# Packing the part numbers of a count build two by two, and moving one table's bias from TensorE to VectorE

## The chip, the cores and the metric

The kernel runs on one core of a Trainium2 chip. Its time is the device time of one execution in microseconds (us). A core has five engines that matter here: TensorE (PE; its weight loads are PEld), VectorE (DVE), ScalarE (ACT), GpSimd (POOL) and SyncE (SP, which only issues transfers). Each engine has a sequencer that reads its instructions, does the register arithmetic itself and passes the rest on to the engine's queue; records of the sequencers carry a q (PEldq, SPq). The engines meet through semaphores.

## The reference

Four graph networks run one after the other on the same graph of 6250 nodes with 256 values each and 100000 edges. The edges are sorted by target. The first network is the one whose first table the change touches:

```python
h = jnp.maximum(_layernorm(x, axis=-1), 0.0)
h = h @ W_in + b_in
for l in range(n_layers):
    agg = jax.ops.segment_sum(h[src], dst, num_segments=n) / deg
    h = jax.nn.relu(agg @ W_agg[l] + h @ W_self[l] + b_hid[l])
return h @ W_out + b_out
```

The kernel folds `W_in` into `W_agg[0]` and `W_self[0]`, so the first table is relu(layernorm(x)) @ (W_in W_agg) + b_in W_agg. The second term is `b_agg`, one row of 256 values that stands in all 128 partitions.

## The kernel before

**The count build.** The sums over edges of five layers are computed as dense products with a matrix of edge counts, `adj`, which is the same in all of them and is built once, in device memory. Rows and columns of the matrix are cut into 784 blocks of 8 target nodes (16 x 392 columns wide when folded onto 128 partitions), and 24 extra parts for blocks with very many edges: 808 parts. The edges come in 782 chunks of 128. Each pair of a chunk and a block that meet is one step, 1592 in all. For a step VectorE makes two one-hot operands, `hot_key` (128 edges x 128 row keys, made for eight steps at a time, L2304) and `hot_j` (128 edges x 392 columns, L2309), and TensorE multiplies them into one of four PSUM banks (L1498). The bank is that of the step's part: part z goes to bank z mod 4. Behind each such matmul TensorE waits until ScalarE has evicted enough parts, and then makes the next bank ready with a small matmul of two columns (L1487). When the last step of a part is done, ScalarE copies its bank into one of eight slots of `staged` (L1723) and SyncE stores the slot into `adj` (L732).

**Registers.** Which part a step belongs to depends on the edges, so it is known only at run time. The numbers lie as one row of 32-bit words, one word a step, in `step_part`, which is a piece of the buffer `g_x` (the profile shows it under that name). TensorE's sequencer loads 16 of them into 16 registers, once at step 0 and once at step 16 of a turn (L1493), and computes from them the bank and the wait (L1494, L1498, L1487). ScalarE and SyncE load eight words each for every eight parts (L1718, L728).

**Turns.** All engines walk the steps in turns of 32 (`build`, through `by_meets`): 50 turns, of which the first, the last two and some of GpSimd's are written out and the others are a loop. Beside the steps each turn does one of the 49 tiles (128 nodes) of the first table, at fixed steps. On TensorE: the transposes `in_T` at step 12, `in_P2` (s_hT times the folded W_agg, into PSUM bank 5) in two halves at steps 29 and 30, the bias as a matmul of a row of ones with `b_agg` behind the second half (L1214), and `in_P3` at steps 1 and 2 of the next turn (L1221). On VectorE: `in_h` at step 4, `in_hT` at step 28, and at steps 18, 20 and 22 of the next turn `in_hi` (L2086: the rounded part of the result), `in_low` (L2065: the rest) and `in_own` (L2070). GpSimd stores the tile at step 28. VectorE may be at most 16 steps ahead of TensorE, since `hot_j` has 16 buffers.

After the build come the dense products (L1352), which TensorE starts when all parts are evicted and the last tile is done.

## Time and profile before

| | |
|---|---|
| median of 3 runs | 7671.14 us (7663.33 to 7676.74) |
| the profiled execution | 7667.53 us |
| its span | 7665.8 us, 108469 instructions |
| TensorE busy | 6321.0 us, 82% of the span |
| VectorE busy | 3412.8 us, 45% |
| ScalarE busy | 1651.3 us, 22% |
| GpSimd busy | 2239.8 us, 29% |
| share of the chain that ended last | TensorE 59%, VectorE 11%, issue 8% |

The span is the profiled execution from its first instruction to its last. Busy times are of the engines, not of their sequencers: an engine whose sequencer is loading a register counts as idle. The build takes about the first 1004 us of the span.

### The profile page before, as it was taken

The numbers are of one execution on the slowest core, as the hardware profiler recorded it, in microseconds if no ns is written. First come the engines' busy times: TensorE is split into PE (matmuls) and PEld (weight loads), VectorE is DVE, ScalarE is ACT, GpSimd is POOL, SyncE is SP. The second block draws the span as 40 slices with busy tenths as digits, with TensorE's granted clock in tenths as the row PEclk, the third lists the DMA queues.
The fourth block names the chain that finished last, engine by engine and source line by source line (L and its number), as shares of the span: only waits on it lengthen the run. The fifth ranks groups of instructions, "written<-read, shape, count | busy, mean of one in ns | idle before, by whom it ended". The sixth has DMA issues, their size and how long they took to land.

```text
span 7665.8 us, 108469 instructions
## 1 busy us (share of the span) xinstructions
PE 6321.0 (82%) x29032; PEld 4993.3 (65%) x29033; DVE 3412.8 (45%) x9453; ACT 1651.3 (22%) x4349; POOL 2239.8 (29%) x2541
## 2 busy tenths in 40 slices
PE   5877799999999999766676765999999966777677
PEld 3555477778887777655555554777787755555555
DVE  7766666661111222355555566122233324444443
ACT  1344410000000111111111113132233332222222
POOL 1000010001001111366666652000111116666664
PEclk8887799999999999878877887999999988878887
DMA  4566777788779777533333336988977753333332
GB/s 138 181 228 242 256 284 261 256 299 312 273 277 343 262 257 256 184 83 83 85 82 84 83 90 200 333 291 294 354 249 244 243 181 97 102 100 99 100 100 75
DMA packets 606869, 1525.79 MB, mean 199 GB/s; under 512 B 72808, under 2 KB 248915, under 8 KB 606612
## 3 DMA queue, kind: packets, MB, share of 16 engines
q1 hardware_dynamic: 472803, 1129.19, 41.8%
q0 software_dynamic: 133824, 393.46, 17.0%
q8 instruction: 143, 2.34, 0.1%
q14 instruction: 99, 0.80, 0.0%
HBM read 1206.47 MB, written 316.80 MB: 199 GB/s over the span
## 4 chain that ended last, share of the span: by engine, by line
PE 59%; DVE 11%; another core or an unknown queue 11%; issue 8%; DMA 6%; DVEq 2%; ACT 2%; SPq 1%; POOL 0%; ACTq 0%; POOLq 0%
PE psum L1352 33%; PE psum L1498 4%; PE psum L1198 4%; PE psum L1646 3%; PE psum L1618 2%; PE psum L1549 2%; DMA slab<-adj 2%; DVE hot_j L2309 2%; DVE acc L2547 2%; DMA g_own<-own_dram 2%; PE psum L1630 1%; PE psum L1537 1%; PE psum L1193 1%; PE psum L1286 1%
## 5 line engine op out<-in xcount | busy, mean ns | idle before, releaser
L1352 PE MATMUL psum<-X,slab 128*128 128x512 f32 x12495 | 3111.2, 402 | 74.9 <-DMA slab<-adj 41.3
L1352 PEld LDWEIGHTS psum<-X,slab 128*128 128x128 f32 x12495 | 2347.7, 191 | 608.5 <-DVE g_x L2374 89.7
L2547 DVE TENSOR_TENSOR acc<-acc,psum 128x264 f32 (+1 forms) x1660 | 702.8, 423 | 1068.8 <-PE psum L1646 353.0
L1498 PE MATMUL psum<-hot_j,hot_key 128*128 128x392 bf16 x1592 | 570.9, 431 | 164.2 <-DVE hot_j L2309 109.4
L1012 POOL DMA_DIRECT2D table<-s_tab x147 | 80.4, 547 | 1910.8 <-DVE s_tab L2065 1910.8
L1537 PE MATMUL psum<-node_tabs,onehot_t 128*128 x1660 | 274.7, 305 | 378.3 <-ACT onehot_t L1822 348.2
L1537 PEld LDWEIGHTS psum<-node_tabs,onehot_t 128*128 128x128 f32 x1660 | 274.0, 248 | 420.6 <-issue 414.3
L1102 POOL DMA_INDIRECT ring<-gat_table,idx_slot x420 | 415.7, 990 | 261.2 <-ACT idx_slot L1817 138.1
L1102 POOL DMA_INDIRECT ring<-rel_table,idx_slot x420 | 412.6, 982 | 250.2 <-ACT idx_slot L1817 137.7
L1723 ACT CAST staged<-psum 128x392 fp32r<-128x392 f32 x808 | 373.0, 489 | 522.3 <-PE psum L1498 497.0
L1498 PEld LDWEIGHTS psum<-hot_j,hot_key 128*128 128x128 bf16 x1592 | 235.7, 148 | 321.7 <-issue 236.2
L2309 DVE TENSOR_SCALAR hot_j<-iota_j,node_tabs 128x392 bf16<-128x392 bf16 x1592 | 411.2, 318 | 73.7 <-PE psum L1498 73.6
L2353 DVE TENSOR_TENSOR node_tabs<-node_tabs,slab 128x896 f32<-128x896 f32 x343 | 374.5, 1092 | 139.2 <-DMA slab<-adj 129.1
L1618 PEld LDWEIGHTS psum<-hT,wbuf 128*128 128x128 f32 x2064 | 383.5, 234 | 48.4 <-ACT hT L1974 2.6
L2065 DVE TENSOR_TENSOR s_tab<-psum,s_tab 128x256 fp32r<-128x256 f32 x196 | 83.1, 424 | 724.3 <-ACT s_tab L1690 724.3
L1618 PE MATMUL psum<-hT,wbuf 128*128 128x128 f32 x2064 | 375.0, 315 | 1.4 <-ACT hT L1974 1.4
L1685 ACT COPY s_hT<-psum 128x256 f32<-128x256 f32 x273 | 101.7, 373 | 1189.5 <-PE psum L1193 1189.5
L1198 PE MATMUL psum<-wbuf,s_hT 128*128 128x256 f32 (+1 forms) x1484 | 336.9, 363 | 0.0
L1487 PE MATMUL psum<-node_tabs 128*128 128x2 bf16 x1593 | 292.7, 184 | 14.2 <-ACT staged L1723 14.0
L1198 PEld LDWEIGHTS psum<-wbuf,s_hT 128*128 128x128 f32 x1484 | 274.9, 190 | 44.4
L1549 PE MATMUL psum<-ring,onehot 128*128 128x264 f32 x840 | 288.9, 481 | 16.7 <-DVE ring L2567 16.7
L1646 PE MATMUL psum<-ring,onehot 128*128 128x256 f32 x840 | 274.0, 420 | 20.6 <-DMA ring<-rel_table,idx_slot 20.3
(426 smaller groups left out, 8124.2 us busy)
## 6 DMA issues: line engine op xcount, KB each, us to landing
slab<-adj SPq DMA_DIRECT2D x383, 1344.0 KB, 6.7
slab<-adj SPq DMA_DIRECT2D x313, 896.0 KB, 6.2
adj<-staged SPq DMA_DIRECT2D x808, 196.0 KB, 1.9
X<-table SPq DMA_DIRECT2D x32, 1792.0 KB, 13.4
table<-s_tab POOLq DMA_DIRECT2D x196, 256.0 KB, 3.5
g_own<-own_dram POOLq DMA_DIRECT2D x35, 896.0 KB, 8.1
own_dram<-s_out POOLq DMA_DIRECT2D x196, 128.0 KB, 5.1
acc<-zero_rows SPq DMA_DIRECT2D x2, 6600.0 KB, 27.4
```

What stands on the lines that cost most here:

```text
L1102: nc.gpsimd.indirect_dma_start(out=to, out_offset=None, in_=tab, in_offset=bass.IndirectOffsetOnAxis(ap=idx_slot[:, r * HALF + u:r * HALF ...
L1198: last = nc.tensor.matmul(ps[:, 0:n], s_hT[:, q, :], w(q), start=(q == 0), stop=(q == Q - 1))
L1352: last = nc.tensor.matmul(sums_of(j), slab[:, slab_at(c), u, j * P:(j + 1) * P], X[:, x_at(p, d), :], start=(d == 0), stop=(d == KT - 1))
L1498: nc.tensor.matmul(psum[:, bass.ds(own, 1), 0:J].rearrange("p o j -> p (o j)"), hot_key[:, s % KEYS // AT_ONCE, :, s % AT_ONCE], hot_j[:, ...
L1537: last = nc.tensor.matmul(ps_log[:, v, :], onehot_t[:, v, :], dst_tab[:, bass.ds(tiles[v], 1), :].rearrange("p t h -> p (t h)"), start=Tru ...
L1549: nc.tensor.matmul(psum[:, v, 0:GW], onehot[:, r * HALF + v, :], homes[r][:, v, :], start=True, stop=True).then_inc(sem("mm"), 1)
L1618: last = nc.tensor.matmul(psum[:, bank, b * P:(b + 1) * P], wbuf[:, q, at:at + P], hT[:, q, :], start=(q == 0), stop=(q == Q - 1))
L1646: nc.tensor.matmul(psum[:, u % GB, 0:D], onehot[:, u, :], homes[r][:, v, 0:D], start=True, stop=True).then_inc(sem("mm"), 1)
L1723: nc.scalar.copy(staged[:, r, :], psum[:, (r + 1) % RING, 0:J]).then_inc(sem("evicted"), 1)
L2309: V.tensor_scalar(hot_j[:, s % HOT, :], iota_j[:], edge_now[:, s:s + 1], None, op0=ALU.is_equal).then_inc(sem("hot"), 1)
L2353: V.tensor_tensor(slab_sum, slab_sum, of[u], ALU.add).then_inc(sem("slab_summed" if u == SIZES[c] - 1 else "slab_partly"), 1)
L2547: V.tensor_tensor(a, a, psum[:, bank, 0:w], ALU.add).then_inc(sem("summed"), 1)
```

## The change

The row of part numbers is packed: the numbers of two steps, which are equal or differ by one, are added into one 16-bit word of a new row `pair_part` (one VectorE operation on one partition, ahead of the build). From a sum s the two numbers come back as s // 2 and (s + 1) // 2. TensorE loads 16 such words once a turn, at step 0, and takes each step's number from them with one more operation on the register.

The bias matmul of the first table goes. In its place VectorE adds `b_agg` to the product as it reads it out of PSUM, into the buffer `s_xn` (new stage `in_sum`, at step 17 of the next turn, ahead of `in_hi`); `in_hi` and `in_low` read `s_xn` then. TensorE's next `in_P2` waits for `in_sum` where it waited for `in_low`.

```diff
+                pair_part = sb("pair_part", [1, PAIRS], I16, scope=late)
...
                     if q == 0:
                         pe.wait_ge(*ev("in_hT", t + 2))
-                        pe.wait_ge(*ev("in_lo", t + 1))
-                    nc.tensor.matmul(PS1_IN, s_hT[:, q, :], cols(W["in", "agg"], D)(q), start=(q == 0), stop=False)
+                        pe.wait_ge(*ev("in_sum", t + 1))
+                    last = nc.tensor.matmul(PS1_IN, s_hT[:, q, :], cols(W["in", "agg"], D)(q), start=(q == 0), stop=(q == Q - 1))
                     if q == Q - 1:
-                        nc.tensor.matmul(PS1_IN, ones[0:1, :], b_agg[0:1, :], start=False, stop=True).then_inc(sem("in_P2"), 1)
+                        last.then_inc(sem("in_P2"), 1)
...
-                    if s % NOW == 0:
-                        pe.load(zs, step_part[0:1, bass.ds(t * BUILD + s, NOW)])
-                    z = pe.snap(zs[s % NOW], min_val=1, max_val=LEAD + ENDED)
+                    if s == 0:
+                        pe.load(zs, pair_part[0:1, bass.ds(t * NOW, NOW)])
+                    if s % 2 == 0:
+                        both = pe.snap(zs[s // 2])
+                    z = pe.snap((both + s % 2) // 2, min_val=1, max_val=LEAD + ENDED)
...
-            pe.wait_ge(*ev("step_part", 16))
+            pe.wait_ge(*ev("pair_part", 1))
...
-                low("in", PS1_IN, 0, t)
+                low("in", s_xn[:], 0, t)
+
+            def in_sum(t):
+                dve.wait_ge(*ev("in_P2", t + 2))
+                dve.wait_ge(*ev("in_lo", t + 1))
+                V.tensor_tensor(s_xn[:], PS1_IN, b_agg, ALU.add).then_inc(sem("in_sum"), 1)
...
-                dve.wait_ge(*ev("in_P2", t + 2))
+                dve.wait_ge(*ev("in_sum", t + 2))
                 dve.wait_ge(*ev("in_tab0", t * 16 + 16))
-                V.tensor_copy(s_tab[:, 0, 0:D], PS1_IN).then_inc(sem("in_hi"), 1)
-
-            in_stages = [(4, in_h), (28, in_hT), (BUILD + 18, in_hi), (BUILD + 20, in_low), (BUILD + 22, in_own)]
+                V.tensor_copy(s_tab[:, 0, 0:D], s_xn[:]).then_inc(sem("in_hi"), 1)
+
+            in_stages = [(4, in_h), (28, in_hT), (BUILD + 17, in_sum), (BUILD + 18, in_hi), (BUILD + 20, in_low), (BUILD + 22, in_own)]
...
+            of_pair = step_part.rearrange("p (n two) -> p n two", two=2)
+            V.tensor_tensor(pair_part, of_pair[:, :, 0], of_pair[:, :, 1], ALU.add).then_inc(sem("pair_part"), 1)
```

Three places in the order of the instructions. The line numbers of the changed kernel are three to ten higher. An ISA row is a register instruction of the sequencer. First TensorE in the body of the loop, from the end of step 15 to the start of step 16, before:

```order
L1498 MATMUL psum<-hot_j,hot_key 128x392
L1487 ISA [waits evicted]
L1487 MATMUL psum<-node_tabs 128x2
L1493 ISA
L1493 TENSOR_LOAD g_x
L1494 ISA
L1498 ISA [waits hot]
```

and the same place after:

```order
L1503 MATMUL psum<-hot_j,hot_key 128x392
L1490 ISA [waits evicted]
L1490 MATMUL psum<-node_tabs 128x2
L1498 ISA
L1503 ISA [waits hot]
```

The load and its set-up are gone; the number of register instructions of a step is the same. Then TensorE at steps 29 and 30 of the loop, before:

```order
L1212 MATMUL psum<-wbuf,s_hT 128x256 [waits tile_lo,tile_hT]
L1494 ISA
L1498 MATMUL psum<-hot_j,hot_key 128x392
L1487 ISA [waits evicted]
L1487 MATMUL psum<-node_tabs 128x2
L1212 MATMUL psum<-wbuf,s_hT 128x256
L1214 MATMUL psum<-pbuf,ones 128x256
L1494 ISA
```

and after:

```order
L1215 MATMUL psum<-wbuf,s_hT 128x256 [waits tile_sum,tile_hT]
L1503 ISA
L1503 MATMUL psum<-hot_j,hot_key 128x392
L1490 ISA [waits evicted]
L1490 MATMUL psum<-node_tabs 128x2
L1215 MATMUL psum<-wbuf,s_hT 128x256
L1498 ISA
```

The bias matmul is gone (each of these rows runs as two matmuls on the array), and the first half waits for `tile_sum`. Last VectorE at steps 16 to 22 of the loop, before:

```order
L2309 TENSOR_SCALAR hot_j<-iota_j,node_tabs 128x392 x2
L2085 ISA [waits tile_P2]
L2086 CAST s_tab<-psum 128x256 [waits tile_tab0]
L2309 TENSOR_SCALAR hot_j<-iota_j,node_tabs 128x392 x2
L2065 TENSOR_TENSOR s_tab<-psum,s_tab 128x256 [waits tile_hi]
```

and after:

```order
L2319 TENSOR_SCALAR hot_j<-iota_j,node_tabs 128x392
L2086 TENSOR_TENSOR s_xn<-psum,pbuf 128x256 [waits tile_lo,tile_P2]
L2319 TENSOR_SCALAR hot_j<-iota_j,node_tabs 128x392
L2095 ISA [waits tile_sum]
L2096 CAST s_tab<-s_xn 128x256 [waits tile_tab0]
L2319 TENSOR_SCALAR hot_j<-iota_j,node_tabs 128x392 x2
L2070 TENSOR_TENSOR s_tab<-s_xn,s_tab 128x256 [waits tile_hi]
```

One operation more, and a wait of VectorE's sequencer on its own engine's result, one `hot_j` behind it.

## Rows read from the trace of the kernel before

**Rows 1.** Timeline of TensorE at the build's two ends: start us, us taken, instruction.

```profile
99.41 1.22 PE L1214 MATMUL psum<-pbuf,ones 1*128 1x256 f32 x2
...
1004.13 0.77 PE L1352 MATMUL psum<-X,slab 128*128 128x512 f32 x1
```

**Rows 2.** Windows: length, busy PE, PEld, DVE, ACT, POOL, PEclk, DMA share, GB/s.

```profile
115.60:599.10 483.50, 395.24 (x2128) 260.91 (x2129) 336.09 (x1207) 187.57 (x397) 31.52 (x57) 0.85 0.53 191
599.10:993.60 394.50, 306.31 (x1512) 191.96 (x1513) 239.94 (x857) 184.97 (x410) 29.58 (x49) 0.76 0.71 251
181.70:190.30 8.60, 6.41 (x40) 4.41 (x38) 7.33 (x27) 1.95 (x4) 1.08 (x2) 0.97 0.42 157
190.30:198.40 8.10, 8.04 (x37) 5.13 (x38) 4.66 (x17) 1.98 (x5) 0.00 (x0) 0.61 0.27 99
```

**Rows 3.** Timeline around the mid load of turn 5: start us, us taken, instruction.

```profile
187.44 0.39 PE L1498 MATMUL psum<-hot_j,hot_key 128*128 128x392 bf16 x1
...
187.79 0.39 PE L1498 MATMUL psum<-hot_j,hot_key 128*128 128x392 bf16 x1
...
188.12 1.01 DVE L2309 TENSOR_SCALAR hot_j<-iota_j,node_tabs 128x392 bf16<-128x392 bf16 x4
...
189.37 1.01 DVE L2309 TENSOR_SCALAR hot_j<-iota_j,node_tabs 128x392 bf16<-128x392 bf16 x4
...
190.36 0.55 PE L1498 MATMUL psum<-hot_j,hot_key 128*128 128x392 bf16 x1 [2.17 <-DVE hot_j L2309]
```

**Rows 4.** Register instructions by source line: duration ns min/median/max, first and last start.

```profile
L1494 PEldq FUSED_REGOPS  x1570: 47/94/108, 100.2 to 1003.6; - x197
...
L1487 PEldq FUSED_REGOPS  x1592: 98/100/124, 100.0 to 1003.7; - x199
```

**Rows 5.** TensorE's register loads, L1493: all of them, then single ones.

```profile
L1493 PEldq TENSOR_LOAD <-g_x x100: 1102/1840/3278, 98.4 to 999.5; - x100
L1493 PEldq FUSED_REGOPS  x47: 47/47/47, 121.9 to 964.0; - x47
...
L1493 PEldq TENSOR_LOAD <-g_x x1: 1912/1912/1912, 188.1 to 188.1; - x1
...
L1493 PEldq TENSOR_LOAD <-g_x x1: 1615/1615/1615, 122.0 to 122.0; - x1
...
L1493 PEldq TENSOR_LOAD <-g_x x1: 1913/1913/1913, 587.2 to 587.2; - x1
...
L1493 PEldq TENSOR_LOAD <-g_x x1: 3278/3278/3278, 607.2 to 607.2; - x1
...
L1493 PEldq TENSOR_LOAD <-g_x x1: 2975/2975/2975, 964.1 to 964.1; - x1
...
L1493 PEldq TENSOR_LOAD <-g_x x1: 1385/1385/1385, 113.9 to 113.9; - x1
...
L1493 PEldq TENSOR_LOAD <-g_x x1: 1752/1752/1752, 617.3 to 617.3; - x1
```

**Rows 6.** Timeline, the bias pair near the head of turn 6.

```profile
197.33 0.69 PE L1214 MATMUL psum<-pbuf,ones 1*128 1x256 f32 x2
```

**Rows 7.** Other register loads by source line: one 16-bit word, six 32-bit words.

```profile
L898 SPq TENSOR_LOAD <-rows_row x83: 3/15/711, 6297.0 to 7621.5; - x83
...
L2823 DVEq TENSOR_LOAD <-turn_row x42: 762/1405/1425, 6298.4 to 7593.6; - x42
```

**Rows 8.** Evictions from 599 to 994 (groups), SyncE's loads, two of SyncE's stores.

```profile
L1723 ACT CAST staged<-psum 128x392 fp32r<-128x392 f32 x410 | 185.0, 490 | 207.8 <-PE psum L1498 185.4 <-DMA adj<-staged 17.2 <-issue 3.1
...
L728 SPq TENSOR_LOAD <-part_to x101: 724/761/1632, 84.8 to 987.2; - x101
...
637.50 0.92 SPq L732 DMA_DIRECT2D adj<-staged  x2
```

**Rows 9.** VectorE operations by source line: duration ns min/median/max, start, form.

```profile
L2086 DVE CAST s_tab<-psum x49: 416/419/422, 105.5 to 978.6; 128x256 fp32r<-128x256 f32 x49
...
L2353 DVE TENSOR_TENSOR node_tabs<-node_tabs,slab x343: 1081/1092/1140, 1005.4 to 1707.7; 128x896 f32<-128x896 f32 x172
```

More of the change, by code:

```diff
@@ L87, in build @@
     assert BTURNS == T + 1 and SB2 * P - MEETS + ENDED + MORE < ELSEWHERE
+    PAIRS = SB2 * P // 2
+    assert MEETS % 2 == 0 and BTURNS * NOW <= PAIRS
     KT = PARTS * DG // P
@@ L505, in build @@
                              ("cuts", 1), ("bound_read", 1), ("cuts_read", 1), ("z_rows", 1), ("parts_out", 1), ("marks", 1), ("x_ve", 1), ("more_rows", 1),
-                             ("b_self", 1), ("rows2_f", 2), ("x_rstd", 1), ("chunk_i", 1), ("edge_f", 2), ("turn_row", 1), ("w_att", 2 * Q),
+                             ("b_self", 1), ("rows2_f", 2), ("x_rstd", 1), ("chunk_i", 1), ("pair_part", 1), ("edge_f", 2), ("turn_row", 1), ("w_att", 2 * Q),
                              ("amax", 1), ("gdiag", 1), ("dst_tab", 1), ("zs_clamped", 1), ("bn_ve", 1), ("bn_shift", 1),
```

2 rows, old and new, of the table TILE_EVENTS are left out of this document.

## The prediction

> **What bounds the kernel now.** I read the page's busy shares first: TensorE 82% of the span, VectorE 45%. So TensorE is the engine to look at, but the share is a mean over stages. The change touches only the count build, the first stage of steps, from 98.3 to 1004.1 us; its last matmuls run straight into the first dense one at 1004.13, with no idle time noted before it [rows 1], so what the build gives up the whole kernel gives up. I then cut the build into its turns of 32 steps. 28 turns fill 115.6 to 599.1 (17.27 us each), the next 20 fill 599.1 to 993.6 (19.73 us each) [rows 2].
>
> What ends last in a turn is not the array but TensorE's sequencer. In a plain stretch one step follows another every 0.35 us (187.44, 187.79) [rows 3]; the sequencer spends 0.094 us and 0.100 us of it on two register instructions [rows 4], and the rest in the spacings around them. It never rests in the first 28 turns. Into this row of small pieces two register loads per turn are set, each of 16 words: one at the turn's head, one at its step 16. While one runs the sequencer passes on nothing. The mid load shows as a hole: the matmul of 187.79 is followed by the next at 190.36, 2.57 us where 0.35 is normal; the load in it took 1.912 us [rows 3, 5]. The row names VectorE's hot_j as what ended the wait, but the four that end at 190.4 are those of steps 28 to 31 (in_hT, which stands ahead of step 28, runs just before them), needed twelve steps later: the load is the cause. The head load is hidden in part: the array still has in_P2's matmuls and the bias pair queued, which runs at 197.33 [rows 6] while the head load of 196.9 is under way.
>
> **Part 1, the mid load goes.** Sixteen packed words now serve 32 steps, so of two loads and two small set-ups per turn one of each goes; the regops per step stay at two (the order shows the same count, one more operand computation inside an existing one). A removed load is worth itself plus 0.16: its set-up of 0.047 [rows 5] and the two spacings around it. Read one by one, the 28 mid loads of the first stretch have a mean of 2.23 us (first 1.615, last 1.913), the 20 of the second 2.55 us (first 3.278, last 2.975); the heads have 1.39 and 1.64 (first of each: 1.385, 1.752) [rows 5]. Sum: 28 x (2.23 + 0.16) = 66.9, 20 x (2.55 + 0.16) = 54.2, and for the first and last turn, 2 x (1.11 + 0.16) = 2.5. Together 123.6 us if nothing takes any of it back.
>
> **Part 2, what takes it back.**
> *Head loads get longer.* The same 16 registers take 1.1 us at best and up to 3.28 [rows 5]. The long ones lie where VectorE runs all through them (from 188.12 to 190.4 it makes eight hot_j with in_hT between [rows 3]); during head loads it mostly waits. VectorE has 12.0 us of work per turn (336.09 / 28) [rows 2]; in a turn of 15 us it is busy 80% of it instead of 70%, and what it used to catch up during the mid load it will catch up during the head load. I take half of the way from head to mid: 0.45 us x 48 = 21.6 us. Bounds: 0, and the whole way, 0.88 x 48 = 42.
> *16-bit words.* Before never loads sixteen of them. Nearest rows: one 16-bit word into SyncE's sequencer, 0.015 us typical; six 32-bit words into VectorE's, 1.405 us, 0.23 a word [rows 7]; sixteen 32-bit words into TensorE's, 1.10 at best. If the bytes count, half of 1.1 is saved, 50 x 0.55 = 27 us; if the registers count, nothing changes. The ends are 27 us gained and, by VectorE's word (sixteen in 3.75 us), 48 x (3.75 - 1.5) = 108 us lost. I take 0, by the row of the same engine.
> *The late turns.* From 599 on, 410 evictions in 394.5 us go through ScalarE (0.49 us each) and SyncE, which issues a store for each, 0.59 us apart at the closest (two of 0.33 in 0.92), and loads its own registers every eight, 0.76 to 1.63 us [rows 8]. 51 octets x (8 x 0.59 + 0.76 to 1.63 + some 0.35 for its loop) = 297 to 342 us. That leaves 53 to 97 us of slack, and the saving would eat 54 of it. The stores have then less room to catch up. Late turns are already 2.5 us longer than early ones though their mid loads are only 0.3 longer: TensorE waits there for other things too. I take 12 us off, bounds 0 and 36.
> *Bias pair.* It goes: two matmuls, 0.69 us together and 0.6 in the array's pace [rows 6], in which the array, not the sequencer, worked; the sequencer passes matmuls on in no time that shows. In the head the array is idle or about to be while the load runs, so taking 0.6 us of array work out of the head makes the hole behind it longer, not the turn shorter. Value 0; bounds 0 and, if the array were the limit in the 20 late turns, 20 x 0.6 = 12 us gained.
> *VectorE's new in_sum.* One more 128x256 operation of 0.42 us per turn [rows 9], some 0.335 of it in the engine's pace, plus some 0.1 for a wait of its sequencer on its own result (hot_j operations are queued behind it and TensorE waits for them four steps later at the soonest, with 8 to 16 steps of lead). 12.0 + 0.43 = 12.5 us in turns of about 15: hidden. If that cover were gone it would cost 0.43 x 49 = 21. in_hi and in_lo now read SBUF; I leave them at their 0.42 [rows 9] (bounds 0 and half of it, hidden either way), so 0.
> *Start.* The packing, 1 partition x 832, is bounded by the 256-element cast, 0.42, and the 896-element addition, 1.09 [rows 9]; I take 0.95, near the addition. It stands ahead of the first hot_j on VectorE, but there the array was busy with in_P2 and the bias (99.41 for 1.22 us) until the first step [rows 1], of which the bias is gone. 0.5 us lost.
> Sum: 123.6 - 21.6 - 12 - 0.5 = 89.5 us. The profiled execution took 7667.5 (span 7665.8 and 1.7 around it), which is 3.6 below the median of 7671.1. 7667.5 - 89.5 = **7578 us**, 1.2% less than before.
>
> **Two rules against the rows.** The Trainium skill, "Runtime: NRT & Kernel Launch", section "Instruction fetch mechanics", puts a register load at some 200 ns for each register even in bulk; by it the shortest load here would be 3.2 us, and the trace has 1.1 us [rows 5], so it is not this price, but its form (registers, not bytes) would make the 16-bit words worth nothing, which is my value.
> In the trace the granted clock was 0.97 in the half turn before the mid load of 188.1 and 0.61 in the one behind it [rows 2], and the matmul went from 0.39 to 0.55 us [rows 3]: the array idled 2.17 us and fell to 1.2 GHz. The Trainium skill, "TensorE: Matmul & The Clock Gate", section "Part 1: The HAM clock gate", says that idling throttles the array and work releases it; the trace agrees, and by it a head hole made longer could lower the clock for the in_P3 matmuls that follow; that is the slow side of the second rival.
>
> **Rivals.**
> R1, nothing is taken back: head loads keep 1.4 to 1.6 and the late turns follow. 123.6 - 0.5 = 123 us less, 7544; with the higher clock after step 16 or shorter 16-bit loads down to 7520. For it: the shortest loads, 1.10, are heads. Against: VectorE's share rises.
> R2, the late turns hardly gain, because eviction and store pace them (or the clock falls at the head and the array lags, which delays evictions): 66.9 + 2.5 - 21.6 - 0.5 and a third of 54 left, 65 us, 7602; with heads as long as mid loads 7622. For it: the 2.5 us by which late turns are longer, and ring buffers of four banks that let TensorE run no more than three parts ahead of ScalarE. Against: at least 53 us of slack.
> R3, VectorE becomes the bound: with the mid load gone its lead is not refilled, and TensorE waits for hot. Price: turns of 15.5 to 16 instead of 14.9, some 40 us of the gain, 7618. For it: 12.5 of 15 us. Against: it idles over 2 us a turn.
> R4, slower: the 16-bit load. Place: the head of each of 50 turns, where the sequencer stands still. If a word costs what VectorE's row says, with 0.3 us to start, a load takes 4.05 us: 2.55 more in 48 turns is 122 against 111 gained (123.6 - 12 - 0.5), so about 7679. It decides from a head load of 3.8 us. Against: SyncE's 16-bit words in 0.015 us [rows 7].
> R5, the change doesn't do what it says: the order shows one load per turn, so only its size is open.
>
> **How the numbers follow.** Forecast (7560 to 7600) 0.48; R1 0.22; R2 0.16; R3 0.07; R4 0.04; the rest, mixtures near no change, 0.03. The range, to leave out at most 2 in 10: from 7530, which keeps most of R1, to 7622, the end of R2. 0.2% is 15 us, about what a measurement of this kernel tells from no change. Faster by more: 0.93; within: 0.03; slower: 0.04.
>
> **What would show it.** Right: one load per turn, starts about 15 us apart in the first 28 turns; no hole at step 16, hot_j matmuls there at 0.39 and a granted clock over 0.9 in the second half turn; head loads of 1.8 to 2.1; 28 turns in about 430 us and 20 in 360 to 370; the dense stage beginning near 915; the rest of the kernel unchanged in length. Wrong: head loads over 3 us (R4); turns of 15.5 and more with TensorE waiting for hot_j (R3); late turns over 19 us with waits for ScalarE (R2); or the dense stage waiting for slabs once the build ends sooner.

## The result, and the profile after

The changed kernel is slower: 7828.94 us (median of 4 runs, 7809.72 to 7832.88) against 7667.24 (4 runs, 7658.87 to 7676.74), a ratio of 1.0206, 95% interval 1.0184 to 1.0227. Forecast were 7578 us, a range of 7530 to 7622, and 0.04 for slower. The profiled execution took 7809.72 us, 142.2 more than that of before. Of these the build itself, from the first step's matmul to the last's, makes 134.7 (903.2 to 1037.9); it begins 2.4 us later (100.6, now 103.0), and what follows the last step is 5 us longer (6662 to 6667).

First the row that answers to [rows 5], then those of [rows 4]. The changed kernel's trace by source line; columns: ns min/median/max, first and last start.

```profile
L1496 PEldq TENSOR_LOAD <-pair_part x50: 3789/4595/6402, 98.7 to 1125.8; - x50
...
L1498 PEldq FUSED_REGOPS  x774: 41/146/165, 103.6 to 1140.2; - x194
...
L1503 PEldq FUSED_REGOPS  x1194: 132/141/162, 102.8 to 1140.8; - x199
its engine sat idle before it (us, times) until:
  issue: 575.4, 619
  DVE hot_j L2319: 3.2, 1
...
L1490 PEldq FUSED_REGOPS  x1592: 98/100/118, 103.0 to 1141.0; - x199
```

There are half as many loads, but the shortest takes 3.79 us and the median 4.6, where the shortest was 1.10 and the median 1.84. The number of these register instructions is the same (3582 in the build, before and after), but one of a step's went from a median of 94 ns to 141 or 146. Under L1503 stands what ended the idle time ahead of the steps' matmuls (us, times): "issue", TensorE's own sequencer, 575.4 us, and `hot_j` 3.2. The same two lines of the kernel before read:

```profile
  issue: 285.8, 414
  DVE hot_j L2309: 109.4, 65
```

The array waits twice as long for its sequencer, and for VectorE no more.

The same windows as [rows 2], turns 1 to 28 and 29 to 48, of the changed kernel: length, busy times of PE, PEld, DVE, ACT, POOL, then PEclk, DMA share, GB/s.

```profile
121.40:677.90 556.50, 407.04 (x2073) 255.75 (x2073) 336.50 (x1232) 187.10 (x397) 31.28 (x57) 0.84 0.46 166
677.90:1131.00 453.10, 327.23 (x1475) 194.68 (x1475) 243.70 (x877) 186.29 (x410) 29.54 (x49) 0.73 0.62 219
```

A turn takes 19.88 us instead of 17.27 in the first 28, and 22.66 instead of 19.73 in the next 20. VectorE and ScalarE are busy for as long as before. How the hole looks, in TensorE's timeline at the head of a turn (start us, us taken, instruction, idle time before it and what ended it):

```profile
190.87 0.68 PE L1215 MATMUL psum<-wbuf,s_hT 128*128 128x256 f32 x2
...
191.58 0.36 PE L1503 MATMUL psum<-hot_j,hot_key 128*128 128x392 bf16 x1
191.78 0.17 PE L1490 MATMUL psum<-node_tabs 128*128 128x2 bf16 x1
196.33 0.54 PE L1503 MATMUL psum<-hot_j,hot_key 128*128 128x392 bf16 x1 [4.38 <-issue]
196.67 0.21 PE L1490 MATMUL psum<-node_tabs 128*128 128x2 bf16 x1
196.74 1.20 PE L1224 MATMUL psum<-wbuf,s_hT 128*128 128x256 f32 x2
```

And windows of the same place: the stretch ahead of the hole, the hole, the two `in_P3` steps behind it, and what follows; under them, in a fence of its own, the `in_P3` steps of the kernel before.

```profile
187.00:191.20 4.20, 3.91 (x22) 2.64 (x22) 4.20 (x17) 1.13 (x3) 0.00 (x0) 1.00 0.52 191
191.20:196.20 5.00, 0.75 (x6) 0.37 (x4) 1.55 (x7) 0.33 (x1) 0.00 (x0) 0.93 0.11 40
196.20:199.20 3.00, 2.87 (x9) 1.90 (x10) 0.00 (x0) 0.49 (x1) 0.00 (x0) 0.50 0.00 0
199.20:203.50 4.30, 4.30 (x28) 2.49 (x27) 3.33 (x12) 1.00 (x3) 0.19 (x1) 0.63 0.25 93
```

```profile
196.80:200.00 3.20, 3.20 (x19) 2.09 (x18) 1.07 (x5) 0.88 (x2) 0.00 (x0) 1.00 0.15 56
```

Two things are to be seen. In the five microseconds of the hole VectorE is busy for 1.55, and 40 GB/s are moved: the load is long with little else going on (VectorE is busy for a mean of 24% of each of the 50 loads). And behind the hole the granted clock is 0.50 (the lower level, 1.2 GHz) where it was 1.00 at the same place before, so that `in_P3`'s pair takes 1.20 us. In steps 0 and 1 of all turns the clock had a mean of 1.00 in the first 28 turns and 0.81 in the next 20; after the change it is 0.52 and 0.50 (means over the turns). In steps 16 to 27 of the early turns it went the other way, from 0.57 to 0.98, and yet these steps take 5.13 us instead of 4.61: the array is faster there and waits for its sequencer.

Measured at the steps' matmuls, a turn splits as follows (mean us from one step's matmul to the next; step 15 carries the old mid load, step 31 the head load):

| steps | before, turns 1-27 | after | before, turns 29-47 | after |
|---|---|---|---|---|
| 28-31, head with load | 3.67 | 6.91 | 4.65 | 8.39 |
| 0-1, `in_P3` | 1.56 | 2.73 | 2.06 | 2.80 |
| 15, mid load | 2.87 | 0.45 | 3.17 | 0.50 |
| 2-14, 16-27 | 9.13 | 9.74 | 9.92 | 10.93 |
| turn | 17.23 | 19.82 | 19.80 | 22.62 |

Times 28 and 20 turns: head +166 us, `in_P3` at the lower clock +48, mid load -121, plain steps +37; together +130 of the build's 134.7.

### The profile page after: what moved, and what is told of

It is laid out like the page before. It is cut to its first block, busy times and chain, and to the rows that moved or that the text cites. A ratio compares the mean times of both kernels' runs of the same rounds, so it can differ in the third digit from the quotient of the medians.

```text
span 7808.0 us, 108317 instructions
## 1 busy us (share of the span) xinstructions
PE 6355.8 (81%) x28934; PEld 4991.3 (64%) x28935; DVE 3417.2 (44%) x9503; ACT 1651.7 (21%) x4349; POOL 2236.9 (29%) x2541
## 3 DMA queue, kind: packets, MB, share of 16 engines
q8 instruction: 145, 2.38, 0.1%
## 4 chain that ended last, share of the span: by engine, by line
PE 58%; DVE 12%; another core or an unknown queue 11%; issue 9%; DMA 5%; DVEq 2%; ACT 2%; SPq 1%; POOL 0%; ACTq 0%; POOLq 0%
PE psum L1355 33%; PE psum L1201 4%; PE psum L1651 3%; PE psum L1503 3%; PE psum L1554 3%; DVE hot_j L2319 2%; PE psum L1623 2%; DMA slab<-adj 2%; DVE acc L2559 2%; PE psum L1635 2%; PE psum L1542 2%; PE psum L1224 1%; PE psum L1196 1%; PE psum L1289 1%
## 5 line engine op out<-in xcount | busy, mean ns | idle before, releaser
L1503 PE MATMUL psum<-hot_j,hot_key 128*128 128x392 bf16 x1592 | 603.5, 425 | 263.1 <-issue 230.7
L1503 PEld LDWEIGHTS psum<-hot_j,hot_key 128*128 128x128 bf16 x1592 | 236.7, 149 | 451.8 <-issue 344.7
L2070 DVE TENSOR_TENSOR s_tab<-psum,s_tab 128x256 fp32r<-128x256 f32 x147 | 62.5, 425 | 725.7 <-ACT s_tab L1695 725.7
L2314 DVE TENSOR_TENSOR hot_key<-iota_keys,key_at 128x1024 bf16<-128x1024 bf16 x199 | 136.6, 686 | 390.4 <-PE psum L1503 389.9
```

The source lines that it names most:

```text
L1503: nc.tensor.matmul(psum[:, bass.ds(own, 1), 0:J].rearrange("p o j -> p (o j)"), hot_key[:, s % KEYS // AT_ONCE, :, s % AT_ONCE], hot_j[:, ...
```

## The experiments

**How they are compared.** The groups of runs (e1 to e4, e5 to e8, e9 to e12, e13 to e15, e16 to e18) ran on different occasions, on three chips, each beside the kernel before: its median was 7610, 7658, 7670, 7616 and, for the last group, 7181 us. The occasion counts and not only the chip, since one chip gave both 7670 and 7181. The difference lies behind the build: from the last step to the end e11 takes 6670 us and e17 6191. Its cause isn't known. So times are compared by their ratios; the build's length and the steps are from one profiled execution each. Where the sequencer sets the pace the steps agree from chip to chip: steps 16 to 27 of the early turns take 5.45 us in e1, in e5 and in e9, which ran on three chips. Lengths where the array works at either clock need not. All variants but e2 and e10 hold TensorE's part number at zero or more with a register operation, `max(number, 0)`; e1 is the control that shows what this costs, and all have such an operation on ScalarE.

| run | what it is | ratio, 95% | build us | load ns min/median/max |
|---|---|---|---|---|
| before | | 1 | 903.2 | 1102/1840/3278 x100 |
| after | | 1.0206 [1.0184, 1.0227] | 1037.9 | 3789/4595/6402 x50 |
| e1 | before + max per step | 1.0140 [1.0119, 1.0160] | 1006.3 | 1102/1631/3297 x100 |
| e2 | after, unsigned words | 1.0205 [1.0183, 1.0226] | 1037.2 | 3789/4604/5986 x50 |
| e3 | after, 32-bit pair words | 1.0035 [1.0022, 1.0048] | 917.5 | 1102/1360/1949 x50 |
| e4 | e1, 16-bit numbers | 1.0546 [1.0523, 1.0569] | 1307.3 | 3793/4822/7001 x100 |
| e5 | e1, one word further on | 1.0539 [1.0522, 1.0557] | 1312.4 | 3799/4852/7207 x100 |
| e9 | e1, two words further on | 1.0536 [1.0519, 1.0554] | 1308.5 | 3798/4746/7580 x100 |
| e6 | e1, one load of 32 words | 1.0091 [1.0071, 1.0110] | 961.7 | 2130/2642/4255 x50 |
| e7 | e1, halves of 32-bit words | 1.0168 [1.0151, 1.0185] | 1017.8 | 1102/1116/1932 x50 |
| e8 | e1, bias on VectorE | 1.0121 [1.0104, 1.0138] | 970.1 | 1102/1634/3115 x100 |
| e10 | e2, bias on TensorE | 1.0201 [1.0184, 1.0218] | 1036.5 | 3790/4590/6311 x50 |
| e11 | e1, both loads moved | 1.0074 [1.0057, 1.0091] | 949.2 | |
| e12 | e11, bias on VectorE | 1.0078 [1.0062, 1.0095] | 946.0 | |
| e13 | e3, shifts for divisions | 1.0155 [1.0134, 1.0175] | 1016.7 | 1102/1140/1855 x50 |
| e14 | e11, max and wait per pair | 1.0088 [1.0063, 1.0112] | 960.3 | |
| e15 | e14, one operation fewer | 1.0087 [1.0070, 1.0105] | 950.2 | |
| e16 | e3, max in a block | 0.9987 [0.9975, 0.9998] | 886.0 | 1102/1381/2197 x50 |
| e17 | e11, max in blocks | 0.9999 [0.9990, 1.0009] | 903.8 | |
| e18 | e17, bias on VectorE | 1.0013 [1.0002, 1.0025] | 903.3 | |

### What makes the load long

**e1_held**, the control.

```diff
+pe.reg_alu(z_held, zs[s % NOW], 0, op=ALU.max)
-z = pe.snap(zs[s % NOW], min_val=1, max_val=LEAD + ENDED)
+z = pe.snap(z_held, min_val=0, max_val=LEAD + ENDED)
```

> The kernel before, with one more register operation on TensorE in each of the 1600 steps of the build (the part number is first held at zero or more: max(number, 0)), and one on ScalarE ahead of its wait, which has slack. It is the control for all kernels derived from the one before, and prices a register operation. Theory A (TensorE's own instruction stream sets the pace of a step, so each register operation counts): 1600 x 0.048 us = +77 us, 7744 us. Rival (a step has slack between its matmuls, an operation more is hidden): 7667 us, no change.

1.0140, some 107 us, more than expected: on TensorE one operation per step, nothing else, and the build is 103 us longer. A plain step has no slack for its sequencer; it goes from 0.35 to 0.43 us. That is some 60 of the 103 us. About 50 more lie in steps 28 to 31, 0 and 1, where the fp32 matmuls run at the lower clock more often (the mid hole gives 10 back): the clock in turns 1 to 28 falls from 0.85 [rows 2] to 0.70:

```profile
116.50:669.00 552.50, 473.92 (x2128) 275.59 (x2129) 335.16 (x1202) 188.22 (x396) 31.40 (x57) 0.70 0.46 167
```

**e2_after_u16**: `pair_part` of type uint16 instead of int16.

> The changed kernel with its 16-bit words unsigned instead of signed (and one register operation more on ScalarE). It is the control for the kernels derived from the changed one. Both theories (16-bit words are read one by one; or the unpacking and the place of the load are the cause): 7829 us within 15, 16-word loads of 4.6 us. Only if the sign extension of a 16-bit word is what costs would it fall, towards 7680 us.

1.0205, as the changed kernel. The sign costs nothing.

**e3_pair32**: the changed kernel with 32-bit pair words.

```diff
-pair_part = sb("pair_part", [1, PAIRS], I16, scope=late)
+pair16 = sb("pair16", [1, PAIRS], I16, scope=late)
+pair_part = step_part[:, 0:PAIRS]              # 32-bit, copied from pair16
...
-both = pe.snap(zs[s // 2])
+pe.reg_alu(z_held, zs[s // 2], 0, op=ALU.max)
+both = pe.snap(z_held)
```

> The changed kernel with its pair words held as 32-bit numbers: the same one load of 16 registers at a turn's head, the same unpacking, and max(word, 0) on each even step (800 register operations more, +40 us by 0.05 each). Theory A (a load costs by how it reads memory, and 16-bit words are read one by one): the load falls from 4.6 us to the 1.4 to 1.6 us of a head load before, 50 x 3.1 = -155, and +40: about 7715 us (7690 to 7740). Rival B (the load is long because of its place at the head, or because of what VectorE and the DMAs do there, and the rest is the unpacking): the load stays at 4 us or more, 7829 + 40 = 7869 us.

The load is back at 1.36 us, the ratio at 1.0035, below e2 by 1.7% although it has 796 register operations more. The place at the head, the packing and VectorE's work in the build are the same in both (one copy of the row ahead of the build is added): rival B falls.

**e4_two_u16**: the control with the numbers as 16-bit words, two loads per turn as before.

```diff
-pe.load(zs, step_part[0:1, bass.ds(t * BUILD + s, NOW)])
+pe.load(zs, step16[0:1, bass.ds(t * BUILD + s, NOW)])      # uint16
```

> The first control (before, number held at zero or more) with one thing changed: the part numbers are 16-bit unsigned words, still one number to a word, 16 words to a load, two loads a turn, no unpacking. Theory A: both loads of a turn take 4.6 us instead of 1.4 to 1.6 and 2.2 to 2.5: (3.1 + 2.3) x 50 = +270 us on the control, about 8014 us if the control is 7744. Rival B (place and unpacking, not the word's width): as the control, 7744 us.

1.0546; expected was 8014/7667 = 1.045. Both loads became long, the mid load more than expected (means 5.25 and 5.88 us). This is the converse of e3: the width alone, without packing, makes the loss.

**e5_shift** and **e9_shift2** ask what a 32-bit load needs to be short.

```diff
-step_part = ...[:, 0:SB2 * P].bitcast(I32)
+step_part = ...[:, 1:1 + SB2 * P].bitcast(I32)        # e5; e9: [:, 2:2 + SB2 * P]
```

> The control (e1_held, 1.014 times the kernel before) with the 32-bit part numbers laid one word further on in memory, so that no load of 16 words begins at a multiple of 16 bytes. Theory A (memory is read in units of four aligned 32-bit words, about 0.27 us each: 16 words are 4 units if they begin on one, 5 if not; a 16-bit word is a unit of its own): both loads of a turn 0.27 us longer, 50 x 2 x 0.27 = +27 us, ratio 1.0175. Rival B (one unit is read for each word unless all is aligned): both loads go to 4 us or more, +250 us, ratio 1.047. Rival C (only the width of a word counts, not where it lies): ratio 1.014, loads as before.

> As e5_shift, with the 32-bit part numbers two words further on instead of one, so that every load of 16 words begins at a multiple of 8 bytes and of no more. Theory A (a load goes four words at a time only where it begins at a multiple of 16 bytes, and word by word at 0.24 to 0.28 us each otherwise): as e5_shift, loads of 4.2 and 5.3 us, ratio 1.054 within 0.003. Rival B (a multiple of 8 bytes lets it go two words at a time): loads of 2.2 and 3 us or so, 50 x 1.9 = +95 us on the control of 1.014, ratio 1.027.

My theory of e5, one unit of four words more, fell: the loads went to 3.80 us and up, as rival B said, and a shift by 8 bytes does the same. The loads by source line, of e1, e4, e5, e9 and e6:

```profile
L1494 PEldq TENSOR_LOAD <-g_x x100: 1102/1631/3297, 96.8 to 1100.6; - x100
```

```profile
L1497 PEldq TENSOR_LOAD <-g_x x100: 3793/4822/7001, 98.1 to 1402.3; - x100
```

```profile
L1494 PEldq TENSOR_LOAD <-g_x x100: 3799/4852/7207, 96.8 to 1406.1; - x100
```

```profile
L1494 PEldq TENSOR_LOAD <-g_x x100: 3798/4746/7580, 98.9 to 1404.3; - x100
```

```profile
L1494 PEldq TENSOR_LOAD <-g_x x50: 2130/2642/4255, 98.1 to 1048.7; - x50
```

Two kinds of load, then. 32-bit words that begin at a multiple of 16 bytes: 1.10 us for 16, 2.13 for 32, 0.067 to 0.069 a word. 16-bit words, or 32-bit words that begin elsewhere: 3.79 to 3.80 us for 16, 0.24 a word. (The 16-bit words begin at a multiple of 32 bytes in e4.) The kernel before shows both kinds for 32-bit words, outside the build: four words of `half_row`, which TensorE reads from a multiple of four words and VectorE from one word further on (its turns begin at word 4i + 1).

```profile
L602 PEldq TENSOR_LOAD <-half_row x44: 303/336/985, 3185.3 to 4528.5; - x44
L602 DVEq TENSOR_LOAD <-half_row x43: 322/966/990, 3197.6 to 4547.5; - x43
```

0.336 against 0.966 us (medians) for four words of the same row: 0.24 a word where the load doesn't begin at a multiple of 16 bytes. VectorE's six words of [rows 7], 0.23 a word, are of this kind too: those loads begin at word 6i + 3. The only one of that line that begins at word 0 has three words and took 0.762 us, so a good place alone may not do for fewer than four words; that wasn't tested.

### Other ways to have one load

**e6_one**: one load of 32 words into 32 registers, no packing.

```diff
-if s % NOW == 0:
-    pe.load(zs, step_part[0:1, bass.ds(t * BUILD + s, NOW)])
+if s == 0:
+    pe.load(zs, step_part[0:1, bass.ds(t * BUILD, BUILD)])
```

> The control (1.014) with one load of 32 aligned 32-bit words at a turn's head into 32 registers, no load in its middle, no unpacking. Theory A: a load costs 0.07 us per word, 16 words more are +1.1 us at the head, of which the queued matmuls there hide about half; the hole in the middle (2.6 to 3.1 us against 0.45 of a step) goes: -2.2 -2.7 +0.6, some -1.8 us a turn, -90 us, ratio 1.002. Rival (what fills the hole is VectorE's or ScalarE's work, which has to be waited for anyway): the time moves to other steps, ratio 1.010 or more.

1.0091, at the rival's end of what was expected. The mid hole went (step 15: 2.56 to 0.50 us) and stayed away; the head, steps 28 to 31 and 0 to 1, took 0.80 us back in the early turns and 1.82 in the late ones.

**e7_halves**: two 16-bit numbers in each 32-bit word, mask or shift in each step.

```diff
+if s % 2 == 0:
+    pe.reg_alu(pair_held, zs[s // 2], 0, op=ALU.max)
+pe.reg_alu(z_held, pair_held, (16 if s % 2 else 0xFFFF),
+           op=(ALU.logical_shift_right if s % 2 else ALU.bitwise_and))
```

> The control (1.014) with two 16-bit numbers to a 32-bit word, one load of 16 aligned words at a turn's head; TensorE takes them apart with one operation in each step (mask or shift) and max(word, 0) in each even step: half an operation per step more than the control. Theory A: the middle load goes (-2.2 to -2.7 us a turn), 16 more register operations cost 16 x 0.06 = +1.0 us: -1.4 us a turn, -70 us, ratio 1.005, and faster than the 32-bit pair words (1.0035) only by its operations, half of one per step (-50 us): between 0.998 and 1.005. Rival (16-bit data, however read, is slow): loads of 4 us, ratio 1.03.

Loads of 1.12 us: 16-bit data read as 32-bit words are read fast. But the time is 1.0168, not 1.005: the steps became 0.46 to 0.69 us long. In each even step two register operations stand alone, of 36 ns each, ahead of the fused ones, and each odd step has a fused instruction of 209 ns. Theory A had the load right and the operations wrong.

### The bias

**e8_bias** is the control with the bias half of the change alone; **e10_after_bias_pe** is e2 with that half undone.

```diff
-pe.wait_ge(*ev("in_lo", t + 1))
+pe.wait_ge(*ev("in_sum", t + 1))
...
-    nc.tensor.matmul(PS1_IN, ones[0:1, :], b_agg[0:1, :], start=False, stop=True).then_inc(sem("in_P2"), 1)
+    last.then_inc(sem("in_P2"), 1)
```

> The control (1.014) with the change's other half alone: the first table's bias is added by VectorE, and the bias matmul goes from TensorE. As predicted (the pair of bias matmuls lies beside the load at the turn's head): ratio 1.014 within 0.002. Theory A (in the control the head load is wholly hidden behind these matmuls, so that a part of the 0.69 to 1.3 us that they take is saved, the rest turns into waiting for the load): -0.5 us a turn, -25 us, ratio 1.0105. Rival (in_sum lies on the way to in_P2 of the next turn and delays it): ratio over 1.016.

> The changed kernel (as e2_after_u16, 1.0205) with the bias matmuls of the first table put back on TensorE: the packed words alone. Theory A (the load of 4.6 us at a turn's head outlasts the matmuls queued ahead of it, so the bias pair of 0.69 to 1.3 us is hidden behind it): ratio 1.0205 within 0.003, the hole at the head shorter by as much as the bias pair is long. Rival (the matmuls and the load do not overlap): +1.0 us a turn, ratio 1.027.

In the changed kernel the bias pair is worth nothing: 1.0201 against 1.0205 for e2, and the steps show why (here beside the changed kernel's). With the pair back, steps 28 to 30 take 0.79 us more (1.80 to 2.59) and step 31 0.81 less (5.11 to 4.30). In the control it may be worth something: 1.0121 against 1.0140, intervals that overlap, with 36 us less in the build, on another chip. Its early turns have 1.37 us less in steps 28 to 31, 0 and 1, half of it in steps 0 and 1 at the higher clock, and 0.60 us more in steps 2 to 14. How much of that is the bias and how much the clock isn't settled.

### Loads out of sight

**e11_moved** issues the loads behind the fp32 matmuls; **e12_moved_bias** has the bias on VectorE besides.

```diff
+if s == 2:
+    pe.load(zs[NOW:BUILD], step_part[0:1, bass.ds(t * BUILD + NOW, NOW)])
+if s == BUILD - 2 and steps == BUILD:
+    pe.load(zs[0:NOW], step_part[0:1, bass.ds(t * BUILD + BUILD, NOW)])
```

> The control (1.014) with its two loads of 16 aligned 32-bit words a turn kept, but issued where TensorE has fp32 matmuls queued: the first half of the next turn's numbers at step 30, behind in_P2, the second half at step 2, behind in_P3; 32 registers, no unpacking. Theory A (the load costs only what outlasts the work queued ahead of it): the hole in the turn's middle (2.6 to 3.1 us against 0.45) goes and no other comes: -2.2 us a turn in the first 28, -2.6 in the rest, -119 us, ratio 0.9985. Rival (the queue ahead of the matmul unit is too short to cover a load of 1.3 us, or the hole was VectorE's work): at least half of the hole comes back at step 2, ratio 1.006 or more.

> As e11_moved, with the first table's bias added by VectorE as in the change. Theory A (with both loads hidden nothing waits for a load at the head, so the bias pair's 1.3 us a turn come back in full at the clock that the turn's head has): -1.0 to -1.3 us a turn, ratio 0.9985 - 0.007 to 0.0085 = about 0.991, under the kernel before although it has one register operation a step more. Rival (in e8_bias only a quarter of what its build gained was left in the whole time): 0.9985 - 0.002 = 0.9965.

1.0074 and 1.0078, where 0.9985 and 0.991 were expected. In e11 step 15 fell by 2.05 us and no new hole came, and yet the early turn is only 1.14 us shorter: steps 2 to 14 rose from 4.93 to 5.54, steps 0 and 1 by 0.36. My reading: in the control the steps behind the head run at the array's pace (0.37 us), because the sequencer had got ahead while the array worked on `in_P3`; a load at step 2 uses that lead up, and the steps run at the sequencer's 0.43 to 0.44 from step 5 on, where in the control they do so from step 13. e12 fits it: 0.78 us less in steps 28 to 30, 0.39 more in step 31 and 0.55 more in steps 2 to 14. So a load behind queued matmuls was not free here; that it spends a lead which the following steps would have used is the likely reason.

### What a register operation costs

**e13_shift**, **e14_pairwait**, **e15_z512**:

```diff
# e13, in e3's steps
-z = pe.snap((both + s % 2) // 2, min_val=1, max_val=LEAD + ENDED)
+pe.reg_alu(z_half, z_half, 1, op=ALU.logical_shift_right)   # after an add in odd steps
+z = pe.snap(z_half, min_val=0, max_val=LEAD + ENDED)
# e14, in e11's steps
+if s % 2 == 0:
+    pe.reg_alu(z_held, zs[s + 1], 0, op=ALU.max)
...
+    pe.wait_ge(sem("evicted"), pe.snap(z_held, ...))         # even steps alone
# e15, in e14's steps
+z512 = pe.snap(z * 512)                                      # used for both matmuls
```

> e3_pair32 (32-bit pair words, one load a turn, 1.0035) with the division by two in each step written as a shift to the right by one; the number of register operations of a pair of steps goes from 5 to 7 (with the copies). Theory A (operations differ in price: a group with a division lasts 140 ns where one without lasts 97, so the division costs some 45 ns more than a mask or shift): 1600 x 0.045 = -72 us, and +16 to +32 us for the copies: -40 to -56 us, ratio 0.997. Rival B (each operation costs the same 0.02 to 0.05 us): +16 to +80 us, ratio 1.0055 to 1.014.

> e11_moved (1.0074) with the holding at zero and the wait for the eviction in each even step alone, for the odd step's number: 800 max operations and 800 waits fewer. Theory A (max costs 0.055 to 0.07 us, as the 152 ns of its group against 83 in the kernel before): -44 to -56 us, ratio 1.001. Rival (the even step now waits for an eviction that is one part later, and this wait is not done yet): ratio 1.0074 or more.

> e14_pairwait with the bank's offset worked out once for both matmuls of a step: the number is multiplied by 512 once, and mask, addition and offset are taken from that: one register operation a step fewer (1600). Theory A (cheap operations, six to a group of 100 ns, cost 0.02 us each): -32 us against e14, ratio 0.997. Rival B (0.05 us each, as the first control's price was reckoned): -80 us, ratio 0.991. Rival C (the pace is not the instruction stream's any more but the matmuls'): as e14.

All three went against theory A; e15 has the ratio of its rival C, but not for its reason: its plain steps of 0.42 to 0.45 us are longer than the array needs even at the lower clock, 0.37. e13 is 1.2% slower than e3, e14 no faster than e11 though it has 796 max operations and waits fewer, e15 no faster than e14 (its group became 10 ns shorter, 90 against 100, and its build 10 us). The rows say what counts. Register instructions of a step, in e3, e13 and e14:

```profile
L1500 PEldq FUSED_REGOPS  x796: 72/164/228, 98.7 to 1015.8; - x199
...
L1506 PEldq FUSED_REGOPS  x1194: 132/141/167, 98.9 to 1016.4; - x199
L1506 PEldq ALU_OP  x398: 32/32/42, 100.0 to 1016.1; - x199
```

```profile
L1501 PEldq FUSED_REGOPS  x796: 114/178/212, 98.5 to 1114.6; - x199
...
L1504 PEldq FUSED_REGOPS  x796: 199/209/222, 99.1 to 1115.2; - x199
...
L1510 PEldq ALU_OP  x1194: 32/32/42, 99.3 to 1115.4; - x199
```

```profile
L1500 PEldq FUSED_REGOPS  x749: 72/173/182, 99.2 to 1059.7; - x188
...
L1508 PEldq MOVE  x796: 29/29/38, 99.5 to 1059.9; - x199
```

A step's operations are packed into fused instructions, and one that isn't packed stands alone, as an ALU_OP. I took six for the most that one holds; no row shows an instruction's contents, and the nearest evidence is e16's block below, 16 operations in three instructions. e3 has an ALU_OP in 398 steps, half of the even ones; in the other even steps a wait splits the group, which also makes an instruction more. Its timeline has the odd and even steps apart:

```profile
193.51 0.39 PE L1506 MATMUL psum<-hot_j,hot_key 128*128 128x392 bf16 x1
193.91 0.39 PE L1506 MATMUL psum<-hot_j,hot_key 128*128 128x392 bf16 x1
194.48 0.36 PE L1506 MATMUL psum<-hot_j,hot_key 128*128 128x392 bf16 x1 [0.18 <-issue]
194.89 0.39 PE L1506 MATMUL psum<-hot_j,hot_key 128*128 128x392 bf16 x1
195.43 0.39 PE L1506 MATMUL psum<-hot_j,hot_key 128*128 128x392 bf16 x1 [0.15 <-issue]
```

0.40 and 0.54 to 0.57 us take turns, and the longer ones wait for issue. e13 has 1194 ALU_OPs, and all its plain steps take 0.56. In e14 a MOVE of 29 ns takes the place of what the missing max saved.

**e16_pair_block**, **e17_moved_block**, **e18_moved_block_bias** put the max behind the load, 16 at once, so that no step has an operation too many.

```diff
 pe.load(zs, pair_part[0:1, bass.ds(t * NOW, NOW)])
+for z_word, word in zip(zh, zs):
+    pe.reg_alu(z_word, word, 0, op=ALU.max)
...
-pe.reg_alu(z_held, zs[s // 2], 0, op=ALU.max)
-both = pe.snap(z_held)
+both = pe.snap(zh[s // 2])
```

> e3_pair32 (32-bit pair words, one load at the turn's head, bias added by VectorE, 1.0035) with max(word, 0) for all 16 words in one block behind the load instead of in the even steps. Theory A (a step's register operations cost what they make of its instructions: six fit in one, and the even step's seventh is an instruction more and 0.17 us): even steps 0.57 to 0.40 us, 16 x 0.17 x 50 = -136 us; the block, three groups, +0.5 to 0.8 us a turn at the head, +25 to +40 us: -96 us, ratio 0.991. Rival B (each operation costs the same wherever it stands): ratio 1.0035.

> e11_moved (two loads a turn behind in_P2 and in_P3, no packed words, bias on TensorE, 1.0074) with the max in blocks of 16 behind each load instead of in each step; no step's group has more operations than in the kernel before. Theory A: steps 0.43 to 0.37 us, 24 of them a turn that the matmuls do not bound, -0.06 x 24 x 50 = -72 us; blocks hidden behind the fp32 matmuls or up to 0.5 us each, +0 to +50 us: ratio 0.998 to 1.004, about 1.000. Rival B (the operations cost the same wherever they stand): 1.0074.

> e17_moved_block with the first table's bias added by VectorE as in the change. Theory A (as in e12_moved_bias against e11_moved: what the bias pair sets free is used up by the blocks and the load, which then stand uncovered): as e17, about 1.000. Rival (the turn's head is bound by the fp32 matmuls, so 0.69 to 1.3 us a turn come back): 0.994.

The rows of e16, first the block, then the lines that were shown of e3:

```profile
L1500 PEldq FUSED_REGOPS  x149: 79/79/148, 91.8 to 968.2; - x149
...
L1502 PEldq FUSED_REGOPS  x727: 47/142/165, 93.2 to 977.9; - x182
...
L1507 PEldq FUSED_REGOPS  x1194: 132/141/162, 92.3 to 978.3; - x199
...
L1505 PEldq ALU_OP  x47: 36/36/42, 108.4 to 929.9; - x47
```

Of the ALU_OPs one a turn is left, behind the load, and the plain step is 0.40 us, even and odd, as forecast. Every fourth step, which begins with the wait for `hot_j`, still takes 0.51 to 0.53, where e3 has 0.54. Steps 16 to 27 went from 5.81 to 5.14 us, in e17 from e11's 5.45 to 4.67 (step 0.43 to 0.36). The same number of operations, moved to another place: rival B falls for both. The whole time came out less good than forecast for e16, 0.9987 against 0.991. The forecast gave each of the 16 even steps of a turn 0.17 us, 136 us in all, but e3 had its ALU_OP in only eight of them, so at most 68 were to be had. And in the early turns steps 28 to 31 did not get shorter (3.90 to 4.27 us) though the array ran its matmuls there at the higher clock (steps 28 to 30 fell from 3.06 to 1.83, step 31 rose from 0.84 to 2.45), so the block and the load stand uncovered there. e16 and e3 are of different occasions; their builds differ by 31.5 us, and their ratios by 0.0048, which is 34 to 37 us. e17 met its forecast (0.9999, expected 1.000). e18 lies at 1.0013: the bias on VectorE gains nothing here either.

e16 is the change as it might have been, with 32-bit words. By the ratios of two groups it is faster than the changed kernel by two per cent, and than the kernel before by 0.13%, which is less than the 0.2% that I take as a difference.

## Why the prediction was wrong

*The mid load goes, 123.6 us.* Right, mechanism and size: step 15 lost 2.42 and 2.67 us, 121 in 48 turns. The granted clock over 0.9 in the second half turn came as well (0.98), but gained nothing, since these steps wait for the sequencer.

*16-bit words, "I take 0, by the row of the same engine".* This step failed. The row of the same engine was of aligned 32-bit words; that words of another width cost as much as words read one by one it could not show. The bound that I had worked out from VectorE's word, 108 us lost, was the true side, and too small: the head, steps 28 to 31, cost 166 us, where the term stood at 0. e3 and e4 show the cause: e4 adds the width alone, and e3 undoes it at the price of an operation; e5 and e9 show that it is one with alignment. The row that I set against the fourth rival, SyncE's 16-bit word in 0.015 us, was of one word into another engine; I took a price for one word as evidence on a bulk load, and a median over records of 3 to 711 ns at that. VectorE's 0.966 us for four words beside TensorE's 0.336 was in the trace: it would have told that there are two prices, 0.24 and 0.08 a word, and that VectorE's 1.405 us in [rows 7] was the higher one. I didn't ask why the two differ. Which of the two 16-bit words would get no row of before could tell.

That was my fourth rival: a head load of over 3.8 us decides for slower. It is 4.4 to 4.9 in the mean. It had 0.04. Its 7679 us was 131 too low: it had neither of the next two terms, 85 us together, and the head grew by 166 us instead of 122.

As for the rule that I set aside, the Trainium skill, "Runtime: NRT & Kernel Launch", section "Instruction fetch mechanics", gives some 200 ns for each register. By the page's own terms those loads are from device memory, while these are from SBUF. The loads of e4, e5 and e9 have 0.24 us a word and agree roughly; the aligned ones have 0.069 and don't. I had dropped it on the shortest load of one kind.

*"The regops per step stay at two".* Their number did stay, but that they would cost the same failed: it counted instructions, not what is in them. The division made the group 141 ns instead of about 94, and the plain steps took 0.61 us more per early turn and 1.01 per late one, 37 us. e1 showed that an operation added to a plain step counts in full.

*The clock behind the head hole.* I wrote of it as the slow side of R2 and gave it no term. It measured +1.17 and +0.74 us a turn in steps 0 and 1, 48 us: the granted clock there was 0.52 and 0.50 in the mean instead of 1.00 and 0.81.

*Head loads get longer, by VectorE's work in them, 21.6 us.* Not what happened. VectorE was idle for most of the hole. In e3, with aligned words and the mid load gone, the head loads had means of 1.26 and 1.52 us against 1.39 and 1.64 before: this term would have been zero or a small gain. Nor does VectorE's work by itself lengthen a load: in e11 14 of the 100 loads ran while VectorE was busy for over 80% of them, and they took 1.10 to 1.29 us.

*The late turns, 12 us.* Not tested by the changed kernel, whose turns are longer. In e3 late turns take 19.48 us against 17.80 early, so even with shorter loads they stay apart; by what wasn't tried.

*Bias pair 0.* Right for the changed kernel (e10 against e2) and for e12 and e18; open for the control (e8). *in_sum hidden.* Right: TensorE waited for `hot_j` once. VectorE's busy time stays at 336 us in the 28 turns; `in_hi`, which was left at 0.42 us, fell to 0.29 with its input in SBUF and pays for a part of `in_sum`. *Start, 0.5 us.* The packing took 1.01 us, but the first load, 3.97 us instead of 1.30, stood uncovered ahead of the first step: 2.4.

## What to carry to other kernels

Where an engine's sequencer sets the pace, count its register instructions and loads as you would matmuls, and price a load by its words' width and where they begin: in loads of 16 and 32, 32-bit words from a multiple of 16 bytes were 0.067 to 0.069 us each; 16-bit words, and 32-bit words from elsewhere, 0.24. A new kind of access has no row in the trace; look for the nearest row that differs in just that property, on whatever engine, before taking the price of the same engine's other kind. And a saved hole is kept only if what pays for it doesn't make another at a place with less cover, since behind the new hole the array may also run at the lower clock.

## What the runs showed of the hardware that was not expected

- A register load of 16 words took 1.10 us at best if 32-bit and from a multiple of 16 bytes; 3.79 us if 16-bit; 3.80 if 32-bit and 4 or 8 bytes off. One word off cost 3.9% of the kernel's time (1.0140 to 1.0539).
- The load at step 16 is longer than the same load at the head, by 0.7 to 0.9 us in e1 (means 1.29 to 1.52 against 1.97 to 2.38) and by 1.0 to 1.3 in e4, 16-bit or not. It isn't shown what lengthens it. VectorE's work by itself doesn't (e11, above), and at step 2 the same words took 1.25 to 1.30 us in the mean (e11).
- A register operation that stood outside the fused instructions made the step some 0.17 us longer (0.40 to 0.57 in e3), more than the 32 ns that its own record shows. A plain operation inside a group took some 10 ns (e15); one with a max added went from a median of 94 to 173 ns (e1), though three instructions with 16 max operations between them took 79 ns each (e16); one with a division by two went from 94 or 98 to 141.
- Loads hidden behind queued matmuls still lengthened the turn (e11), through steps that no longer ran ahead.
